# Doubled scratch for delta and u, the first group's delta and u by halves, unread products on TensorE at the start, and the experts' bias rows made in the last group

## The reference, cut to what matters

```python
h = concat([cls, patches @ W + b], 1) + pos ; h = concat([h, txt], 1)
# selective scan on the layer-normed tokens, width 512, 16 states
xz = ln(h) @ W_in ; x, z = split(xz)
x = silu(conv4(x) + conv_b)
dt, B, C = split(x @ W_x)
delta = softplus(dt @ W_dt + b_dt)
state = exp(delta * A) * state + (delta * x) * B     # over 114 tokens, 512 channels x 16 states
y = (state . C + x * D) * silu(z)
h = h + y @ W_out
# gated feed-forward for every token; for 512 tokens also the best of 8 experts
s = ln(silu(n @ sw1 + sb1) * (n @ sw2 + sb2)) ; shared = s @ sw3 + sb3          # n = ln(h)
e = ln(silu(m @ ew1 + eb1) * (m @ ew2 + eb2)) * sel_g + sel_b ; expert = e @ ew3 + eb3
out = h + shared ; out[512 chosen tokens] = h + w0 * shared + w1 * expert[argmax]
```

## Time and profile before

| | |
|---|---|
| time, median of 3 runs | 1781.32 us (1778.06 to 1785.29) |
| the profiled execution | 1780.39 us, span 1778.0 us |
| VectorE busy | 1582.9 us, 89% |
| GpSimd busy | 1569.1 us, 88% |
| TensorE busy | 1475.8 us, 83% |
| ScalarE busy | 1329.4 us, 75% |
| mean granted TensorE clock | 0.929 of full speed |

### The profile page before, as it was taken

How to read it: one execution, slowest core, us unless ns; L and a number is a source line. 1 busy time by engine, 2 the same in 40 slices (tenths; PEclk the granted TensorE clock), 3 DMA queues, 4 the chain that set the end, 5 groups by cost and what they waited for, 6 DMA issues and landing times.

```text
span 1778.0 us, 27104 instructions
## 1 busy us (share of the span) xinstructions
PE 1475.8 (83%) x9464; PEld 1039.4 (58%) x9464; DVE 1582.9 (89%) x1387; ACT 1329.4 (75%) x3100; POOL 1569.1 (88%) x782
## 2 busy tenths in 40 slices
PE   7768888888887888888988888888888888887588
PEld 6545656555655656556666655666565656554355
DVE  2589999999999999999999999999999999999935
ACT  2577788787887888787777878878787888786644
POOL 1689999999999999999999999999998999998804
PEclk9888999998999999999998989999998999996899
DMA  3767755555666555656575555666655555656110
GB/s 112 149 129 190 155 128 114 122 120 131 136 131 141 127 125 116 127 121 146 120 152 122 119 114 125 136 135 132 141 128 117 117 126 127 137 117 137 35 34 15
DMA packets 194138, 217.94 MB, mean 123 GB/s; under 512 B 93979, under 2 KB 184485, under 8 KB 193490
## 3 DMA queue, kind: packets, MB, share of 16 engines
q1 hardware_dynamic: 193234, 215.04, 55.1%
q0 software_dynamic: 576, 1.17, 0.3%
q10 hardware_dynamic: 192, 0.01, 0.0%
HBM read 169.92 MB, written 46.62 MB: 122 GB/s over the span
## 4 chain that ended last, share of the span: by engine, by line
POOL 30%; DVE 30%; issue 15%; ACT 12%; PE 11%; DMA 2%; SPq 1%; DVEq 0%; ACTq 0%; POOLq 0%
POOL xr L1629 18%; DVE psum L1302 12%; DVE xr L1302 12%; POOL xr L1637 10%; ACT psum L1005 4%; DVE xr L1311 2%; PE psum L789 2%; DVE vv L1373 2%; PE psum L613 2%; PE psum L790 2%; ACT soft L1053 1%; ACT soft L1057 1%; PE psum L704 1%; ACT soft L1061 1%; ACT L1127 1%
## 5 line engine op out<-in xcount | busy, mean ns | idle before, releaser
L1629 POOL TENSOR_TENSOR xr<-u,bbc 128x912 f32<-128x912 f32 x512 | 1078.9, 2137 | 15.0 <-DMA u<-u_scratch 15.0
L1005 ACT ACTIVATE psum<-delta,a_neg 128x228 f32<-128x228 f32 x2048 | 805.6, 440 | 216.4 <-DVE xr L1311 184.8
L1302 DVE TENSOR_TENSOR_SCAN psum<-psum,xr 128x912 f32<-128x912 f32 x320 | 655.8, 2049 | 66.3 <-ACT psum L1005 54.6
L1637 POOL TENSOR_TENSOR xr<-xr,cbc 128x912 f32<-128x912 f32 x192 | 408.5, 2128 | 35.4 <-DVE xr L1302 32.5
L1302 DVE TENSOR_TENSOR_SCAN xr<-psum,xr 128x912 f32<-128x912 f32 x192 | 392.1, 2042 | 0.0
L718 PE MATMUL psum<-xr,fold 128*32 128x228 f32 x4096 | 299.2, 390 | 85.4 <-POOL xr L1637 59.0
L1311 DVE TENSOR_TENSOR xr<-psum,cbc 128x912 f32<-128x912 f32 x320 | 353.6, 1105 | 11.5 <-DVE psum L1302 0.5
L613 PE MATMUL psum<-xh,win 128*128 128x228 f32 x1024 | 227.6, 372 | 64.1 <-ACT xs L1036 33.5
L613 PEld LDWEIGHTS psum<-xh,win 128*128 128x128 f32 x1024 | 195.6, 196 | 95.8 <-ACT xs L1036 44.2
L718 PEld LDWEIGHTS psum<-xr,fold 128*32 128x32 f32 x4096 | 97.4, 113 | 222.3 <-issue 85.7
L668 PE MATMUL psum<-xi,conv_d 128*128 128x228 f32 x1024 | 210.9, 358 | 0.0
(11 more groups left out here) (201 smaller groups left out, 1656.3 us busy)
## 6 DMA issues: line engine op xcount, KB each, us to landing
delta<-delta_scratch SPq DMA_DIRECT2D x256, 228.0 KB, 6.4
u<-u_scratch SPq DMA_DIRECT2D x256, 228.0 KB, 4.2
bbc<-bc_scratch SPq DMA_DIRECT2D x128, 114.0 KB, 2.5
u_scratch<-u SPq DMA_DIRECT2D x64, 228.0 KB, 4.8
cbc<-bc_scratch SPq DMA_DIRECT2D x128, 114.0 KB, 2.7
delta_scratch<-delta SPq DMA_DIRECT2D x64, 226.0 KB, 5.6
out<-ob SPq DMA_DIRECT2D x32, 228.0 KB
h_scratch<-h SPq DMA_DIRECT2D x31, 228.0 KB
```

Source lines behind the costliest of these rows:

```text
L1005: ins = nc.scalar.activation(slot(k)[:, j * TOK:(j + 1) * TOK], delta4[:, c // 2, j, c % 2], ACT.Exp, scale=a_neg[:, c, j, n:n + 1])
L1302: nc.vector.tensor_tensor_scan(x if k in ON_POOL else slot(k), slot(k), x, 0.0, ALU.mult, ALU.add).then_inc(scan_done, 1)
L1629: nc.gpsimd.tensor_tensor(xr[:, k % XRING], u4[:, c // 2, :, c % 2], bbc[:, p, n].unsqueeze(1).to_broadcast([P, J, TOK]), ALU.mult).then_i ...
L1637: nc.gpsimd.tensor_tensor(xr[:, k % XRING], xr[:, k % XRING], cbc[:, p, k % NI].unsqueeze(1).to_broadcast([P, J, TOK]), ALU.mult).then_inc ...
```

## The change

There are four parts. First, `u_scratch` and `delta_scratch` get a second copy, used by odd groups; the first fill of `delta_scratch` (L583) is done for both, by four DMAs where there were two; SyncE's stores wait for the loads of two groups before, and `delta_out` and `u_out` wait for the store of the group before (out of SBUF) where they waited for its loads. Second, for group 0 VectorE makes the halves of delta and the first half of u ahead of `image_tokens(1)`, GpSimd the second half of u, and SyncE stores and loads half 0 ahead of half 1. Third, TensorE runs products that nobody reads: 12 before the first tokens, 4 between `center(0)` and `var(0)`, 6 after `var(0)`. Fourth, the small expert constants on GpSimd move to the start of group 6, `bias_rows` to unit 13 of group 31, the add that ends them to VectorE's `after_last`, and a few pieces behind the last group change places.

The scratch, and SyncE's stores and loads:

```diff
+    u_scratch = nc.dram_tensor("u_scratch", (2, 2, J, DQ, 2 * TOK), F32, kind="Internal").ap()
+    delta_scratch = nc.dram_tensor("delta_scratch", (2, 2, J, DQ, 2 * TOK), F32, kind="Internal").ap()
...
+                    def keep_u(g, half):
+                        need(sp, u_in[half], 16 * NQ * (g - 1))
+                        rows = u_scratch[g % 2, half].rearrange("j d x -> (j d) x")
                         sp.dma_start(rows, u[:, 2 * half:2 * half + 2].rearrange("p c t -> p (c t)")).then_inc(u_out_s[half], 16)
...
+                    def keep_delta(g, half):
+                        need(sp, delta_in[half], 16 * NQ * (g - 1))
+                        rows = delta_scratch[g % 2, half].rearrange("j d (z t) -> (j d) z t", t=T)
+                        sp.dma_start(rows[:, :, 1:],
...
+                    def spread_u(g, half):
                         sp.wait_ge(u_out_s[half], 16 * (g + 1))
-                        spread(u_scratch, u4, half, u_in)
-                        sp.wait_ge(delta_out_s[half], 16 * (g + 2))
-                        spread(delta_scratch, delta4, half, delta_in)
+                        spread(u_scratch[g % 2, half], u4, half, u_in)
+                    def spread_delta(g, half):
+                        sp.wait_ge(delta_out_s[half], 16 * (g + 3))
+                        spread(delta_scratch[g % 2, half], delta4, half, delta_in)
...
-                            keep_delta(half)
-                        for half in range(2):
+                            keep_delta(0, half)
                             sp.wait_ge(u_done, 1 + half)
-                            keep_u(half)
-                        for half in range(2):
-                            spread_tensor(0, half, delta_scratch, delta4, delta_out_s, 32, delta_in)
-                            spread_tensor(0, half, u_scratch, u4, u_out_s, 16, u_in)
+                            keep_u(0, half)
+                            spread_delta(0, half)
+                            spread_u(0, half)
                             if half == 0:
                                 rows_out(cbc, 0, NS, c_in)
...
+                    for a in range(2):
+                        for half in range(2):
+                            sp.dma_start(delta_scratch[a, half].rearrange("j d x -> (j d) x"),
+                                         delta[:, 2 * half:2 * half + 2].rearrange("p c t -> p (c t)")).then_inc(delta_out_s[half], 16)
```

TensorE: the bias rows in group 31, the unread products, and the order behind the last group:

```diff
+                    def bias_rows():
+                        pe.wait_ge(ew_in, EW_IN)
+                        pe.wait_ge(pool_c, 4)
+                        pe.wait_ge(sz_done, 2 * GROUPS)
+                        for x in range(E):
+                            mm = pe.matmul(psum[0:E, CB, 0:DM], selb_e[:, x], e3[:, x], start=(x == 0), stop=(x == E - 1))
+                        mm.then_inc(eb3_mm, 1)
...
+                            if i == GROUPS - 1 and k == 13:
+                                bias_rows()
                             if runs(i):
                                 reduce_states(i, k)
...
+                    def idle_turns(n):
+                        for _ in range(n):
+                            pe.matmul(psum[:, YB, 0:P], mean_w[:], mean_w[:], start=True, stop=True)
                     def first():
+                        pe.wait_ge(const_pool, CONST_POOL)
+                        idle_turns(12)
                         pe.wait_ge(token_in, TOKEN_IN)
                         tokens(0, 1)
                         pe.wait_ge(const_dve, DVE_TOKENS)
                         center(0)
+                        idle_turns(4)
                         var(0)
+                        idle_turns(6)
...
-                    pe.wait_ge(ew_in, EW_IN)
                     v_center(ga)
                     h2_turn(gz)
                     v_var(ga)
-                    bias_rows()
                     ffn_in(gz)
+                    turn_rows(0)
                     ffn_out(ga)
-                    turn_rows(0)
                     v_center(gz)
                     turn_rows(1)
+                    hidden(0, 0)
                     v_var(gz)
-                    hidden(0, 0)
                     turn_rows(2)
                     turn_rows(3)
```

VectorE: the first delta and u, the wait of `delta_out`, and the add of the bias rows, moved from behind `expert_rows(1)`:

```diff
+                    def first_delta(half):
+                        lo, hi = 2 * half, 2 * half + 2
+                        dve.wait_ge(spl_done, 1)
+                        dve.wait_ge(delta_out_s[half], 32)
+                        nc.vector.scalar_tensor_tensor(out=delta[:, lo:hi], in0=dt_bank(half), scalar=0.0, in1=soft[:, lo:hi],
+                                                       op0=ALU.max, op1=ALU.add).then_inc(delta_done, 1)
+                        if half == 0:
+                            dve.wait_ge(delta_done, 1)
+                            dve.wait_ge(xs_done, 2)
+                            nc.vector.tensor_tensor(u[:, lo:hi], delta[:, lo:hi], xs[:, 0, lo:hi], ALU.mult).then_inc(u_done, 1)
...
-                            need(dve, delta_in[half], 16 * NQ * g)
+                            dve.wait_ge(delta_out_s[half], 16 * (g + 2))
...
+                            first_delta(half)
                         image_tokens(1)
-                        delta_out(0)
                         means_out()
...
+                        dve.wait_ge(eb_in, EB_IN)
+                        dve.wait_ge(eb3_mm, 1)
+                        nc.vector.tensor_tensor(eb3x, psum[0:E, CB, 0:DM], eb3r, ALU.add).then_inc(eb3_done, 1)
...
+                    expert_stats(0)
                     v_norm(ga)
-                    expert_stats(0)
```

GpSimd: `u_out`, and the expert constants in group 6 (their five instructions and waits are unchanged):

```diff
+                        if g == 0:
+                            pool.wait_ge(u_done, 1)
+                            nc.gpsimd.tensor_tensor(u[:, 2:], delta[:, 2:], xs[:, p, 2:], ALU.mult).then_inc(u_done, 1)
+                            return
                         for half in range(2):
-                            need(pool, u_in[half], 16 * NQ * g)
+                            need(pool, u_out_s[half], 16 * g)
                         nc.gpsimd.tensor_tensor(u[:], delta[:], xs[:, p], ALU.mult).then_inc(u_done, 2)
...
+                        if i == 6:
+                            expert_constants()
```

More of the change, by code:

```diff
@@ L466, in keep_delta, with spread @@
                                      ).then_inc(delta_out_s[half], 16)
-                    def spread(scratch, dst, half, done):
-                        rows = scratch[half].rearrange("j d x -> d j x")
+                    def spread(rows, dst, half, done):
                         for q in range(NQ):
                             sp.dma_start(dst[q * DQ:(q + 1) * DQ, half].rearrange("p j c t -> p j (c t)"),
-                                         rows).then_inc(done[half], 16)
-                    def spread_half(g, half):
+                                         rows.rearrange("j d x -> d j x")).then_inc(done[half], 16)
@@ L484, in rows_out, with spread_half @@
+                    def spread_delta(g, half):
+                        sp.wait_ge(delta_out_s[half], 16 * (g + 3))
+                        spread(delta_scratch[g % 2, half], delta4, half, delta_in)
+                    def spread_half(g, half):
+                        half_free(g, half)
+                        spread_u(g, half)
+                        spread_delta(g, half)
                     def rows_out(buf, p, lo, done):
@@ L489, in rows_out @@
                                          rows.partition_broadcast(DQ)).then_inc(done, 16)
[L491 to L495, removed]
                     def before_first():
@@ L552, in body @@
                                 sp.wait_ge(delta_done, 2 * i + 3 + half)
-                                keep_delta(half)
+                                keep_delta(i + 1, half)
                             for half in range(2):
                                 sp.wait_ge(u_done, 2 * i + 3 + half)
-                                keep_u(half)
+                                keep_u(i + 1, half)
                             spread_half(i + 1, 0)
@@ L581, in _ @@
                     sp.wait_ge(const_pool, CONST_POOL)
-                    for half in range(2):
-                        sp.dma_start(delta_scratch[half].rearrange("j d x -> (j d) x"),
-                                     delta[:, 2 * half:2 * half + 2].rearrange("p c t -> p (c t)")).then_inc(delta_out_s[half], 16)
+                    for a in range(2):
+                        for half in range(2):
+                            sp.dma_start(delta_scratch[a, half].rearrange("j d x -> (j d) x"),
+                                         delta[:, 2 * half:2 * half + 2].rearrange("p c t -> p (c t)")).then_inc(delta_out_s[half], 16)
                     def experts():
@@ L926, in turn_hot @@
                         mm.then_inc(hot_mm, 1)
-                    def bias_rows():
-                        pe.wait_ge(pool_c, 4)
-                        for x in range(E):
```

(4 more changed lines are left out.)

29 lines of the change are left out of this document (10 added, 19 removed).

## The result

Over 20 runs each the kernel took 1780.51 us before and 1776.60 us after (1768.85 to 1781.66), a ratio of 0.9973 with a 95% interval of 0.9961 to 0.9985: 2.7 to 6.9 us faster, under the 0.5% line. The forecast was 1773.2, 8.1 us faster; the sign was right and the size twice too large. The 1776.60 lies inside the stated range (1767 to 1781), 0.6 us above the part of it that had a chance of 0.50 (1770.5 to 1776), and nearer to rival (a)'s 1778 than to the forecast.

The account below looks back on a forecast made before the run. It took the loop of 32 groups as bound by VectorE's and GpSimd's scans and multiplications; -4.9 - 0.7 - 3.0 + 0.2 + 0.3 = -8.1 us gave 1772.3 profiled, 1773.2 for the median, range 1767 to 1781.

Parts of the forecast that it names:

- rival (a): At the start, the clock rises early but loads keep the patches at 71 to 73 us; about 1778, chance 0.20.
- What bounds it: The 32 groups are a loop of about 50 us, held by scans and multiplications on VectorE and GpSimd.
- Part 1, 0 us: In the loop, the waits loosened by two scratch copies were over long before, so 0 us.
- Part 3, -4.9 us: At the start, unread products raise TensorE's clock early; group 0's softplus ends at 35.6 rather than 40.48: -4.9 us.
- Part 2, -0.7 us: In group 0, halves let the first loads go out earlier and the patches land at 67.6 us: -0.7 us.
- Part 4, -3.0: Behind the last group, moving the bias rows and reordering pieces brings the gates 3.0 us earlier; bounds -3.55 and -1.5.
- Part 4, +0.2 in group 31: Bias rows lose some 1.7 to 2 us; the output projection returns 1.7 through the raised clock: +0.2 us.
- Part 4, +0.3 in group 6: GpSimd's five small instructions now stand in the loop, costing between 0 and 0.7 us: +0.3 taken.

Follow-up runs that it names:

- c_no_halves: The changed kernel without group 0's halves, all four stores ahead of all loads as before; 0.9965 of before.
- b_stores_first: The changed kernel with SyncE issuing the stores of both halves of group 0 ahead of the first loads; 0.9949 of before, 1772.55 us.
- b_patches_early: The changed kernel with the patches of groups 2 and 3 issued behind half 1's stores, ahead of SyncE's wait for them; 0.9929 of before.
- d_all_late_turns: The changed kernel with group 0's stores first, patches early, bias rows at unit 12, and unread products in two more group 31 waits; 0.9925 of before, 1766.72 us.
- a_scratch_only: The kernel before with only the second copy of both scratches and its waits; 0.9979 of before.
- d_scratch_again: The kernel before with only the second copy of both scratches and its waits, run again on another occasion and chip; 1.0008 of before.
- a_tail_scratch: The kernel before with the scratch copies and the fourth part, without products at the start and without halves; 0.9984 of before.

## Why the prediction was right in sign and twice too large

- **What bounds it.** Right in the main: a group in which the clock stays up takes 50.2 us in both traces. But the loop is not held by VectorE and GpSimd alone; see the end of this section.
- **Part 1, 0 us.** Not refuted: 0.9979 and 1.0008 for the same kernel.
- **Part 3, -4.9 us.** Right in each figure: the tokens end at 11.95 for a forecast of 12.2, the projection takes 3.32 us, the softplus ends at 35.57 for 35.6.
- **Part 2, -0.7 us, and what of part 3 passes the patches.** This is the term that was mis-sized, in three places. Half 0's round trip was put at 4.0 us and took 5.09, so its loads went out at 41.56 and not at 40.2. Half 1's stores were to land 1.7 us behind the loads, which puts half 1's loads at 53.5; the store took 8.79 us, and the loads went out at 56.27. That the patches still landed at 68.4, only 0.8 us behind the forecast's 67.6, is luck: from half 1's loads on it took 12.2 us, where the sum had 14.1. So the patches came 4.8 us earlier than before and the softplus 4.9, and part 2 is about +0.1 up to there. The third place is a cost that the sum left out: the tokens took 5.94 us for 4.86 before. In both kernels the clock was down when they began, but here it came back 5.6 us after their start (at 74.1) and before 3.4 us after it. VectorE went on 3.7 us earlier instead of 5.6. The comparison of c_no_halves with the changed kernel says that the halves are worth about 0; b_stores_first and b_patches_early show what held them: the order of SyncE's queue.
- **Part 4, -3.0.** From the end of the output projection to VectorE's first gate instruction it took 26.95 us before and 25.10 after: -1.8. The step's working fits where the clock stays up: in d_all_late_turns the stretch is 23.50 us, -3.4. In the changed kernel's profile the clock was at half speed from 1698.8 to 1702.3, and the output products of group 29 took 1.6 us longer. The forecast left this possibility out, as it took the clock behind the last group for granted.
- **Part 4, +0.2 in group 31.** y 2.0 us late, the projection 2.4 us shorter: -0.4. The mechanism was right. One reading was not: in the trace of before the clock stood at 1.00 when TensorE came to that place (1683.9) and fell at 1684.3; in the trace after it was down from 1678.4 to 1685.2.
- **Part 4, +0.3 in group 6.** Nearly right: the five instructions stand from 369.44 to 370.08 and cost 0.47 us. From GpSimd's u of group 6 to its u of group 7 the eight profiled kernels that have them there take 50.64 to 50.67 us, the six others 50.17 to 50.19. GpSimd's idle time before u (1.11 us, and 1.09 in the kernel before) doesn't take them up. In all eight, one multiplication on VectorE (L1400 in the kernel after, the norm's last step) takes 1.54 to 1.57 us in that group, and 1.08 to 1.10 in the six; why is open.

```profile
369.44 0.10 POOL L1681 MEMSET half_neg<- 128x8 f32 x1
...
369.93 0.19 POOL L1688 CAST prio<-prio_i 128x8 f32<-128x8 int32 x1
...
392.20 2.13 POOL L1678 TENSOR_TENSOR u<-delta,xs 128x912 f32<-128x912 f32 x1 [1.11 <-issue]
```

The profiled pair adds up: -3.7 at the start, +0.8 in the loop, -2.2 behind the last scan, -5.1 in span. Of the 0.8, 0.47 are the constants of group 6. The timed pair says -3.9. Of the rivals, (a) came nearest: the clock rises and the patches keep part of the gain; but they landed at 68.4, not at 71 to 73.

The loop itself differs by up to 8 us between executions of one kernel (a_scratch_only and d_scratch_again), and the forecast had nothing for that. The 14 profiled executions show what goes with it. Take the time from one u on GpSimd to the next, for the groups 3 to 30: 378 lengths. In 150 of them the clock was at 0.50 for at most 1.2 us, and 149 of these last 50.17 to 50.21 us (the last one has the constants of group 6). In 152 of the 378 the group takes over 50.8 us, up to 53.2, and in each of these the clock was at 0.50 for 3.4 us or more; in the 77 over 52 us, for 12.8 us or more. Time at half clock need not cost anything: most groups with about 10 us of it take 50.2 us too. One group shows where it does:

| group, from u to u | length | granted clock | `proj_delta`, 8 records | VectorE idle before delta |
|---|---|---|---|---|
| a_tail_scratch, 295.44 to 345.63 | 50.19 | 0.90 | 1.77 us | none |
| c_no_halves, 287.89 to 340.40 | 52.51 | 0.87 | 3.38 us | 2.22 us |

In c_no_halves the clock was down from 329.5 to 339.7, under TensorE's last step ahead of the softplus, so that delta and the scans behind it came late; in a_tail_scratch it was down at other times. So a gain of a few us at the start is carried through the loop only up to such steps, which come at other groups in each execution: the kernel after was 3.7 us ahead of before at u of group 1, 0.5 at group 4, 5.5 at group 21 and 3.2 at group 31.

## What to carry to other kernels

Where one engine issues stores and loads in turn, issue the stores first, and put a transfer that is wanted first (here the patches) into the round trip of the one whose answer you must await: the wait for half 1's store was 8.8 to 9.7 us in the kernels that had issued loads ahead of it. Splitting work in halves was worth nothing until the queue's order followed. Where TensorE waits at the start and at the end of a kernel, products that nobody reads are cheap if they stand in idle time, and they are worth what the clock gives to the work right behind them. Before a change of a few us is measured, look at how much the loop differs between two executions of the same kernel.

## What the runs showed of the hardware

- The granted clock rose at 9.2 us with the 12 products, which began at 3.79, and at 25.4 without them; with it up, the following 24 records of 72 columns took 2.67 us for 5.40.
- It also rose under products with only 8 columns of weights: in the kernel after the bias rows began at 1681.29, 0.8 us behind 4.1 us of idle time, and the clock rose at 1685.2.
- A store of 226 KB took 5.1 us to its landing with little in the queue, and 8.8 us behind 2.3 MB of loads, half of which had moved when it was issued. In the kernel after the DMA engines then moved 14 GB/s from 55.0 to 56.3 us, with half 1's loads not yet issued.
- A group of the loop takes 50.2 us while the clock is up and up to 53.2 us when it is down at the wrong place (378 groups of 14 executions).
- One kernel, two occasions on chips of the same kind: 0.9979 and 1.0008 of the kernel before, each with an interval of about 0.0015 on either side.
